# Attention in a megakernel: the order within two key chunks, statistics tile by tile, and seven banks for the last scores

## The reference

```python
x = x + _L0_xattn_ref(_layernorm(x), ctx, ...)   # softmax, 16 heads of 16, 1601 keys
x = x + _L0_ffn_ref(_layernorm(x), ...)
x = x + _L1_xattn_ref(_layernorm(x), ctx, ctx, ...)   # autocorrelation
x = x + _L1_ffn_ref(_layernorm(x), ...)
x = x + _L2_xattn_ref(_layernorm(x), ctx, ctx, ...)   # sigmoid(q k / 4) @ v, no sum
x = x + _L2_ffn_ref(_layernorm(x), ...)
x = x + _L3_xattn_ref(_layernorm(x), ctx, ...)   # softmax
x = x + _L3_ffn_ref(_layernorm(x), ...)
```

```python
scores = jnp.einsum('bhqd,bhkd->bhqk', q, k)
attn = jax.nn.softmax(scores, axis=-1)
ctx = jnp.einsum('bhqk,bhkd->bhqd', attn, v)
```

## Time and profile before

| | us |
|---|---|
| median of 3 runs | 3026.52 |
| lowest and highest | 3020.13, 3045.28 |
| the profiled execution | 3022.72 |
| its span | 3020.7 |
| PE busy | 2813.9 (93%) |
| DVE busy | 1633.8 (54%) |
| ACT busy | 1593.5 (53%) |
| POOL busy | 291.9 (10%) |

### The profile page before, as it was taken

How to read it: one execution, slowest core, us unless ns; L and a number is a source line. 1 busy time by engine, 2 the same in 40 slices (tenths; PEclk the granted TensorE clock), 3 DMA queues, 4 the chain that set the end, 5 groups by cost and what they waited for, 6 DMA issues and landing times.

```text
span 3020.7 us, 38820 instructions
## 1 busy us (share of the span) xinstructions
PE 2813.9 (93%) x14660; PEld 1417.8 (47%) x14660; DVE 1633.8 (54%) x2980; ACT 1593.5 (53%) x2688; POOL 291.9 (10%) x233
## 2 busy tenths in 40 slices
PE   7999999998799889998999999979989999999987
PEld 3434344443477757775333333367633434434323
DVE  5777777775475364431112121046476777777805
ACT  1677777777300111111687877831247677677752
POOL 2010100000101011220001010031201000010000
PEclk7899999999899999999999999989979999999976
DMA  5432242330300001001653545020133423423100
GB/s 109 66 44 47 35 52 45 44 45 1 90 1 28 1 15 49 1 1 45 99 61 59 74 53 58 1 83 1 29 43 50 54 46 44 66 26 41 23 4 29
DMA packets 68951, 125.51 MB, mean 42 GB/s; under 512 B 20976, under 2 KB 45464, under 8 KB 65312
## 3 DMA queue, kind: packets, MB, share of 16 engines
q1 hardware_dynamic: 67616, 120.61, 26.1%
q10 hardware_dynamic: 1152, 2.44, 0.3%
HBM read 42.47 MB, written 2.10 MB: 15 GB/s over the span
## 4 chain that ended last, share of the span: by engine, by line
PE 80%; DVE 8%; ACT 6%; issue 3%; DMA 1%; SPq 1%; ACTq 1%; POOL 0%; POOLq 0%; DVEq 0%
PE psum L190 52%; PE psum L687 20%; PE psum L1809 6%; DVE mpart L872 5%; ACT probs L752 4%; PE psum L275 1%; PE psum L1802 0%; DVE prod L1592 0%; DVE x L1305 0%; DVE stats L302 0%; ACT qp_lo L740 0%; DMA qst<-qp_lo 0%; DVE cross L1599 0%; PE psum L706 0%; ACTq L983 0%
## 5 line engine op out<-in xcount | busy, mean ns | idle before, releaser
L752 ACT ACTIVATE probs<-psum 128x512 f32<-128x512 f32 (+3 forms) x2080 | 1283.5, 691 | 402.6 <-PE psum L190 400.7
L872 DVE TENSOR_REDUCE mpart<-psum 128x2 f32<-128x804 f32 x1024 | 980.4, 992 | 339.6 <-PE psum L190 334.2
L190 PE MATMUL psum<-qst,kst 50*128 50x512 f32 (+3 forms) x2496 | 671.2, 466 | 29.7 <-ACT probs L752 17.1
L687 PE MATMUL psum<-probs,vt 128*17 128x512 f32 (+1 forms) x4992 | 683.5, 621 | 0.5 <-ACT probs L752 0.5
L190 PEld LDWEIGHTS psum<-qst,kst 50*128 50x128 f32 (+3 forms) x2496 | 288.1, 187 | 542.6 <-issue 324.3
L190 PE MATMUL psum<-kst,qst 48*128 48x402 f32 x2048 | 437.4, 425 | 49.5 <-DVE mpart L872 45.0
L190 PEld LDWEIGHTS psum<-kst,qst 48*128 48x128 f32 x2048 | 210.5, 196 | 345.6 <-DVE mpart L872 187.5
L190 PE MATMUL psum<-wv,ctxT 128*128 128x256 f32 (+1 forms) x624 | 188.3, 432 | 5.4 <-ACT hT L289 4.3
L190 PE MATMUL psum<-ctxT,wk 128*128 128x512 f32 (+1 forms) x384 | 158.2, 542 | 23.5 <-DMA ctxT<-in_ctxT 22.4
L687 PEld LDWEIGHTS psum<-probs,vt 128*17 128x17 f32 (+1 forms) x4992 | 83.6, 96 | 183.4 <-issue 150.4
L190 PEld LDWEIGHTS psum<-wv,ctxT 128*128 128x128 f32 (+1 forms) x624 | 113.6, 201 | 61.3 <-issue 34.5
(11 more groups left out here) (281 smaller groups left out, 2786.9 us busy)
## 6 DMA issues: line engine op xcount, KB each, us to landing
kst<-kp_hi SPq DMA_DIRECT2D x144, 200.1 KB, 5.8
ctxT<-in_ctxT SPq DMA_DIRECT2D x36, 512.0 KB, 5.0
kst<-kp_lo SPq DMA_DIRECT2D x72, 200.1 KB, 5.4
qst<-qp_hi SPq DMA_DIRECT2D x144, 64.0 KB, 4.5
kst<-kp_hi SPq DMA_DIRECT2D x84, 100.1 KB, 2.9
qst<-qp_lo SPq DMA_DIRECT2D x72, 64.0 KB, 5.1
kst<-kp_lo SPq DMA_DIRECT2D x42, 100.1 KB, 3.0
stage<-in_L_ffn_W SPq DMA_DIRECT2D x16, 256.0 KB, 4.6
```

The source lines that it names most:

```text
L190: last = e.matmul(dst, lhsT, rhs, start=i == 0, stop=i == len(pairs) - 1)
L687: t = e.matmul(c.bank(self.acc)[32 * h:32 * h + VW, :], self.vt[0:kn, kc, self.head(g, h), :], p[0:kn, h % self.wide, :], start=kc == 0, s ...
L752: e.activation(self.probs[n % slots][0:kn, :, :], c.psum[0:kn, k:k + self.wide, :], ACT.Exp if softmax else ACT.Sigmoid, scale=DH ** -0.5) ...
L872: e.tensor_reduce(self.mpart[:, :, p * (SEQ // P) + qt, i], c.psum[:, k:k + 2, 0:MAX_WIDTH], AX.X, ALU.max).then_inc(c.drained(k), 1)
```

## The change

The letters of the sigmoid cycle bring the two scores steps of each chunk together, and the other work ahead of or behind them; the last cycle puts its two products together. With softmax the step w moves ahead of the maximum that stood before it. In the fourth unit of a batch the value steps begin at the third cycle instead of the second. The four tiles' statistics are four steps instead of two. With softmax the scores from chunk 10 of unit 14 to the end, behind the last maximum, go round seven banks instead of three.

```diff
--- before.py
+++ after.py
@@ -49,8 +49,8 @@
 PROBS = 16
 
 
-CYCLE = "swsvsxsv", "ssmwmssvssmxmssvmm"
-LAST_CYCLE = "wsvsxv", "wssvmsxsmv"
+CYCLE = "wssvxssv", "sswmmssvssmxmssvmm"
+LAST_CYCLE = "wssvvx", "wssvmsxsmv"
 VW = DH + 1
 
 E0, E1, E2, E3 = 8, 4, 8, 16
@@ -250,8 +250,9 @@
         self.c = c
 
     def steps(self, f, b):
-        return [("n_stats", f, b, 0), ("n_stats", f, b, 2), ("n_power", f, b), ("n_root", f, b),
-                ("n_rows", f, b, 0), ("n_rows", f, b, 2), ("idle",), ("n_turn", f, b, 0), ("n_turn", f, b, 2)]
+        return [("n_stats", f, b, i) for i in range(4)] + [
+            ("n_power", f, b), ("n_root", f, b), ("n_rows", f, b, 0), ("n_rows", f, b, 2), ("idle",),
+            ("n_turn", f, b, 0), ("n_turn", f, b, 2)]
 
     def hT_made(self, f, b):
         k, v = self.c.at(("n_turn", f, b, 2))
@@ -298,11 +299,10 @@
             i = step[3]
             if i == 0:
                 e.wait_ge(*x_final(c, f - 1, b))
-            for t in range(4 * b + i, 4 * b + i + 2):
-                a = c.dve.count(e.bn_stats(c.stats[:, t, :], c.x[:, t, :]))
-                e.wait_ge(c.dve.sem, a)
-                a = c.dve.count(e.bn_aggr(c.meanvar[:, t, :], c.stats[:, t, :]))
-            self.moments = a
+            t = 4 * b + i
+            a = c.dve.count(e.bn_stats(c.stats[:, t, :], c.x[:, t, :]))
+            e.wait_ge(c.dve.sem, a)
+            self.moments = c.dve.count(e.bn_aggr(c.meanvar[:, t, :], c.stats[:, t, :]))
         elif kind == "n_power":
             e.wait_ge(c.dve.sem, self.moments)
             e.tensor_scalar(c.veps[:, ts], c.meanvar[:, ts, 1], LN_EPS, None, ALU.add).then_inc(c.sem("var_made"), 1)
@@ -442,13 +442,16 @@
                 steps += [self.query_steps(b + 1)[0:1], self.query_steps(b + 1)[1:2], keys[0][0:1], keys[0][1:2]][i - 3]
         elif g == 2 and i < 4 and b + 1 < BATCH:
             steps += [keys[0][2:4], keys[1][0:1], keys[1][1:2], keys[1][2:4]][i]
-        elif g == 3 and i and b + 1 < BATCH:
-            steps += self.value_steps(b + 1, *((i - 1, i) if i < 5 else (4, 6) if i == 5 else (6, 7)))
+        elif g == 3 and i > 1 and b + 1 < BATCH:
+            steps += self.value_steps(b + 1, *((0, 1), (1, 3), (3, 4), (4, 6), (6, 7))[i - 2])
         others = {(0, 5): ("ctx", f, b + 1), (2, 1): ("half", f, 4 * b + 4, 0), (2, 4): ("half", f, 4 * b + 4, 1)}
         if (g, i) in others and b + 1 < BATCH:
             steps.append(others[g, i])
         return steps
 
+    def behind_maxima(self, step):
+        return self.softmax and step[2:4] >= (UNITS - 2, 10)
+
     def max_steps(self, u):
         return [("max", self.f, u, p, qt, i) for p in range(HALVES) for qt in range(SEQ // P) for i in range(MAX_SPLIT)]
 
@@ -458,7 +461,7 @@
         if softmax:
 
             scores = misc = turns = first_values = Ring(0, 1, 2)
-            maxima, prelude = Ring(4, 6), Ring(4, 5, 6, 7)
+            maxima, prelude, tail = Ring(4, 6), Ring(4, 5, 6, 7), Ring(0, 1, 2, 4, 5, 6, 7)
         else:
             scores, misc, turns, first_values = Ring(0, 2, 4), Ring(7), Ring(0, 1, 2), Ring(7, 3)
             maxima, prelude = None, Ring(3, 4, 5, 7)
@@ -469,8 +472,8 @@
             placed.extend(spread(steps, begin, end))
 
         if 0 in mine:
-            put(self.norm.steps(f, 0)[:6], -3.7, -3.6)
-            put(self.norm.steps(f, 0)[7:], -2.45, -2.4, turns)
+            put(self.norm.steps(f, 0)[:8], -3.7, -3.6)
+            put(self.norm.steps(f, 0)[9:], -2.45, -2.4, turns)
         for b in mine:
             if b:
                 put(self.norm.steps(f, b), GROUPS * (b - 1) + 0.05, GROUPS * (b - 1) + 0.9, misc)
@@ -500,6 +503,9 @@
             put(steps, u, u + 1, misc)
             ring.update((step, scores) for step in steps if step[0] == "scores")
             ring.update((step, maxima) for step in steps if step[0] == "max")
+            if softmax:
+
+                ring.update((step, tail) for step in steps if step[0] == "scores" and self.behind_maxima(step))
             if u + 2 < UNITS and (u + 2) % GROUPS:
                 put([("unit", f, u + 2)], u + 0.02, u + 0.02)
         for b in range(BATCH):
@@ -527,6 +533,10 @@
                 if second not in seconds:
                     seconds.add(second)
                     self.beside[step] = second, c.visits[second]
+            elif kind == "scores" and self.behind_maxima(step) and c.at(step)[0] in (5, 7):
+
+                first = c.at(step)[0] - 1
+                self.beside[step] = first, c.visits[first]
             if kind in ("keys", "query"):
 
                 kind = "early" if self.early(step) else "late"
```

## The result

The changed kernel takes 3002.05 us in the median of 9 runs (2997.46 to 3015.74), the kernel before 3029.71 (9 runs beside them). The ratio is 0.9915, 95% interval 0.9892 to 0.9938: faster by a little under 1%. The forecast was 3013 us and "within 1%", with a range of 2985 to 3038.

A forecast was written before the change was run, and what follows sets the result against it. PE was taken to bound the attentions, except the sigmoid's last units (ACT full) and the softmax's last unit (neither full). Sigmoid -19, values -6, statistics -6, banks +21 make -10 on 3022.7: 3013 us, range 2985 to 3038.

The forecast's parts named there:

- the seven banks: Softmax tails: waiting for the exp just before empties ACT, +21 us (bounds -3.5 and +34).
- The walk through seven chunks: Softmax tails at 2.4 GHz: stepping through the new order gives 3.21 us a chunk instead of 2.65; 2.06 without second wait.
- the clock falls in both tails: Softmax tails: PE waits of 1 to 2 us bring 1.2 GHz in two chunks of three.
- Rival 2: Both softmax tails keep full clock, 2988 us; chance 0.17.
- the sigmoid step: Sigmoid attention: joining split scores makes half cycles with a value step 2.71 us; -19 us in all (bounds -12 and -21).
- the seventh cycle's saving: Sigmoid attention, last cycle of a unit: two groups fewer save 0.28 us in each of 13 units, 3.6 us.
- the one sentence on the DMAs: Query and key steps only change place within the cycle, and DMAs on SP's queue stay behind the same steps; no size given.
- "0" for the softmax letters: Softmax cycles with work in w: as many changes between groups as before, so 0 us.
- rival 1: Softmax cycles with w: maxima in pairs become the bound, 28 us uncovered, 3041 us; chance 0.13.
- values later and statistics: Softmax attention: later value steps remove ACT's wait, -6 us; single-tile statistics remove PE stalls before maxima, -6 us.
- "elsewhere 0": Feed-forward phases: the two extra statistics steps shift norms by a few places, 0 us (-2 to +2).

The follow-up runs named there:

- the one-wait variant: Changed kernel, but the first scores on bank 5 or 7 wait once for the last maximum, later ones only for their own bank; 2944.54 us, ratio 0.9710.
- the banks apart: Changed kernel with the second wait kept, but the seven banks in the order 4, 6, 0, 5, 7, 1, 2; 2951.91 us, ratio 0.9732.
- the strings alone: Kernel before with only the sigmoid cycle's new step order, last cycle included; 3021.49 us, ratio 0.9968.
- statistics in pairs, spread: Kernel before with two idle places added among the norm steps, two tiles' statistics still running together; 3023.60 us, ratio 0.9980.

## Why the prediction came out as it did

**Right: the seven banks cost.** The step was "a second wait in front of banks 5 and 7, for the exp just before". It was forecast at +21 us with bounds of -3.5 and +34; alone it measures +0.76%, in the changed kernel 29 us. In the two profiles compared above the tails grew by 32.9 us; 12.7 of it is that the kernel before had kept its clock in one of them. The trace shows the waits, the one-wait variant removes them and 57 us, and with the banks apart the second wait is nearly free. The walk through seven chunks that priced it (2.06 against 3.21 us) is also what made the better kernel plain: without the holes ACT is the bound, and its 8.93 us for 18 exps are 0.496 each.

**Right: the clock falls in both tails.** 0.71 and 0.67 were granted. The waits there reach 1.58 us. That it fell because of them is not shown: in the second profile of the kernel before, waits like the 0.52 of the earlier trace rows were followed by a tail of 0.71 too, and so was the second tail in both profiles. What the runs show is the other direction: where the second wait was needed once or the banks stood apart, all eight tails of four profiles had 0.86 to 0.91. The Trainium skill's rule on long pauses (TensorE: Matmul & The Clock Gate, HAM oscillation) does not describe this: the low clock came with no such pause. The Trainium skill's section "A second HAM failure mode: psum-queue depth-cycling" on the same page has the clock swing when PE idles briefly but often between groups of matmuls; the trace agrees, with 0.71 and 0.67. Rival 2, for which the first rule spoke, did not occur.

**Right: the sigmoid step, with a part given back.** Half cycles went from 2.89 to 2.71 us as worked out, and the seventh cycle's saving was 0.27 in the first unit where I took 0.28. That the stage lost 20.0 us against 19 is in part luck: the strings alone took away 14, the values alone 4.4 (450.7 us), the statistics alone 3.4 (451.7 us). What the step missed is the one sentence on the DMAs: they do "stay behind the same steps", but their landing does not move with PE, and one wait grew from 1.5 to 5.3 us.

**Wrong: "0" for the softmax letters.** I counted changes between kinds of matmul and maxima that wait for each other. I did not ask which step stands behind the one that waits: the work step can be done while DVE is late, the maximum cannot. Measured 0.51%, about 15 us, of which that reason covers the 3.2 us of PE's idle time; most of the rest in layer 3 is the clock, as the table below has it. That the pair of maxima would wait instead (rival 1) did not show: PE's idle time before maxima was 41.8 us in that kernel, 45.0 before.

**Wrong in size: values later and statistics.** Each was forecast at 6 us; alone they measure 0.53% (16 us) and 0.80% (24 us). The direction was right, but I priced only the wait itself, and what PE itself waited was less than I took: 3.0 us for the value copies against 6, and 5.5 us less before maxima with the split (45.0 to 39.5) against 6. The gain came by another way. Three adjoining stretches of layer 3, end of unit 2 and start of unit 3, in the kernel before (columns as in the earlier trace rows):

```profile
2322.00:2361.70 39.70, 37.95 (x237) 14.59 (x235) 30.00 (x37) 30.40 (x60) 4.16 (x4) 1.00 0.42 51
2361.70:2372.00 10.30, 9.80 (x36) 3.82 (x38) 4.58 (x5) 4.88 (x10) 0.00 (x0) 0.50 0.89 103
2372.00:2410.00 38.00, 37.43 (x231) 16.73 (x233) 28.77 (x35) 27.84 (x55) 0.00 (x0) 1.00 0.21 23
...
2367.24 0.38 ACT L775 ACTIVATE vt<-psum 128x256 f32<-128x256 f32 x1 [4.16 <-PE psum L687]
```

The last line is the value copy among them, which waits 4.16 us. PE had 1.2 GHz for 10.3 us, and did 36 matmuls in them where it does about 62 at full clock (237 in 39.7, 231 in 38.0). So 10 us at 1.2 GHz lose about 4, an estimate from these lines. Three more such stretches stood in this attention ahead of its tail, 10.2 us at 2269.6, 6.8 at 2539.3 and 6.8 at 2587.0, and the second profile of the kernel before has all four again. The trace's granted clock gives the time at 1.2 GHz in the attention of layer 3 up to unit 14:

| kernel | stage, us | at 1.2 GHz, us |
|---|---|---|
| before, both profiles | 617.4 | 37.2 and 37.1 |
| statistics in pairs, spread | 615.7 | 37.1 |
| softmax letters | 609.5 | 22.4 |
| statistics tile by tile | 610.9 | 21.1 |
| values later | 607.4 | 16.9 |
| the changed kernel | 603.6 | 16.5 |

Each of the three edits alone takes away 15 to 20 us at 1.2 GHz, by the estimate 6 to 9 us of the 6.5 to 10.0 by which the stage shortened, and all together take away 20.7, hardly more than the values alone. In the five profiles of kernels with none of the three edits the time at 1.2 GHz is 31 to 37 us, in the six with all of them 16 to 27. That the wait of the value copy makes the clock fall is refuted for this place. The fall at 2361.7 comes before the copy waits; with the letters or the split alone the copies wait as before (14.0 and 16.8 us in all), yet the clock there is full; and the changed kernel, in which no copy waits for a product, has 1.2 GHz there for 6.8 us. What does make it fall stays open.

**Doubtful: "elsewhere 0" for the statistics.** The stretch between the first two attentions took 664.1 to 672.8 us in the seven profiles of kernels with the split and 671.7 to 677.6 in the seven without it. The means, 667.6 and 674.4, are 7 us apart, but six of the seven have the other edits too. With the split alone it is 669.8, with the places alone 671.7, and one kernel differs by 6.8 us from profile to profile here. So "0" is not refuted beyond doubt in this stretch, and no wait of that size was found.

**The sum.** The four edits apart from the banks were forecast at -31 us and measure 0.9822, 54 us; the banks were forecast at +21 and cost 29. The two errors lie on opposite sides. The sum also started from 3022.7 us, where the median of 9 runs beside the changed kernel is 3029.7; that hid 7 us more. So the total of 3002 lies 11 us from the forecast, 1 us below the forecast's own 3003 to 3023 and inside the wide range, closer than its parts deserve. What stays open, beside what moves the clock: how much of each single variant's gain is a tail that happened to keep its clock. The profiles of the softmax string, the values and the statistics have one tail each of 68.8 to 70.3 us and one of 75.6 to 82.9, and their single ratios add up to 2.2% where the four together give 1.8%, which would fit edits that take away the same time at 1.2 GHz.

## What to carry to other kernels

When buffers are added behind a shared counter, write down which count the new wait names: a count that includes the step just issued turns seven buffers into a handshake, and the fix, or just moving the two buffers apart in the ring, was worth as much here (57 and 50 us) as all the rest of the change (54). In an order written by hand, put behind a step that may wait one that needs nothing from the late engine. And read the granted clock of a stage beside its time: a small reorder here was worth more through the time at 1.2 GHz than through the wait it took away, and two such edits need not add up.

## What the hardware showed beyond that

The same tail of the same kernel took 70.2 us or 82.9: at a granted clock of 0.91 or 0.71, with 13 waits of PE for ACT before scores in both, 6.0 us in the first and 4.6 in the second. With the engines' work closed up (one wait), the tail stayed at 61.8 to 63.6 us, both tails in all three profiles. Two pairs of scores, each alone ahead of other work, hold PE 0.19 us longer than the four together (0.43 twice against 0.67). Two products in a row take 1.84 us up to the next scores (1473.37 to 1475.21 in the changed kernel), two apart 0.98 each.
